# Gated values split in fp16 by channel scales and turned by DMAs instead of TensorE, with the forward transform in fp16 and the filling in another order

## What is computed

```python
# x: (8, 512, 512); in_proj_w: (1536, 512); wq_gate, wq_up: (1408, 512) int32; wq_down: (512, 1408) int32
u = transpose(x @ in_proj_w.T + in_proj_b, (0, 2, 1))
uc = depthwise_conv(u, short_w, taps=3, causal)[..., :512] + short_b
x0, x1, v = split(uc, 3, axis=1)
k = filter_k(...)                  # small sine network over positions, (512 channels, 512)
v = v * x1                         # "the gated values"
y = irfft(rfft(v, 1024) * rfft(k, 1024)) + v * filter_bias
y = transpose(y * x0, (0, 2, 1))
x = layernorm(x + y @ out_proj_w.T + out_proj_b)
gate, up = silu(qlinear(x, wq_gate)), qlinear(x, wq_up)
return layernorm(x + qlinear(gate * up, wq_down))
```

## Time and profile before

| | before |
|---|---|
| median of 3 runs (lowest to highest) | 991.51 us (990.58 to 991.9) |
| the profiled execution, own time | 990.85 us |
| its span | 989.0 us |
| busy: TensorE, VectorE, ScalarE, GpSimd | 96%, 77%, 44%, 56% of the span |
| granted TensorE clock, mean | 0.995 |
| first matmul of the first `gu` | 126.5 us |
| DMA, mean over the span | 48 GB/s |

### The profile page before, as it was taken

One profiled execution on the slowest core, in us unless ns is written; L12 is line 12 of the kernel. 1 busy time (PEld: TensorE's weight loads), 2 busy tenths in 40 slices (PEclk: granted clock), 3 DMA queues, 4 the chain that ended last, 5 costly groups with the idle time before them and its releaser, 6 DMA issues.

```text
span 989.0 us, 17316 instructions
## 1 busy us (share of the span) xinstructions
PE 951.5 (96%) x6121; PEld 666.5 (67%) x6210; DVE 763.5 (77%) x1441; ACT 436.7 (44%) x940; POOL 555.5 (56%) x628
## 2 busy tenths in 40 slices
PE   6798999999999999999999999999999999999996
PEld 3345667767676776767676676767767676787774
DVE  6698897787878788787887778787887878686454
ACT  4577543434344344534444343443445344334342
POOL 0269885474747656474765647475564747575210
PEclk9999999999999999999999999999999999999998
DMA  9444400221101211221012211012111110101100
GB/s 289 144 128 131 105 1 1 44 64 22 44 12 32 65 23 43 43 59 24 6 44 43 64 23 44 11 33 65 22 44 23 43 22 6 39 1 44 44 21 22
DMA packets 98953, 47.97 MB, mean 48 GB/s; under 512 B 80048, under 2 KB 84784, under 8 KB 98868
## 3 DMA queue, kind: packets, MB, share of 16 engines
q1 hardware_dynamic: 98370, 46.79, 18.2%
q10 hardware_dynamic: 498, 0.08, 0.0%
HBM read 32.17 MB, written 8.39 MB: 41 GB/s over the span
## 4 chain that ended last, share of the span: by engine, by line
PE 74%; DVE 9%; issue 6%; POOL 4%; ACT 3%; POOLq 0%; DVEq 0%; ACTq 0%
PE gate_up L1315 12%; PE gate_up L1316 12%; PE bank L1158 9%; PE bank L1160 9%; PE bank L1159 9%; PE down L1328 7%; PE down L1327 5%; PE bank L1275 4%; DVE tmp L1067 2%; PE spectrum L1158 1%; PE spectrum L1159 1%; PE spectrum L1160 1%; POOL acc L878 1%; DVE hid_lo L1146 1%; ACT cx L779 1%
## 5 line engine op out<-in xcount | busy, mean ns | idle before, releaser
L884 POOL TENSOR_TENSOR acc<-acc,tmp 128x256 f32<-128x256 f32 x160 | 122.5, 766 | 137.2 <-DVE tmp L1067 125.1
L1067 DVE TENSOR_TENSOR tmp<-spectrum,filt 128x512 f32<-128x512 f32 x256 | 172.7, 680 | 0.0
L830 ACT ACTIVATE hid<-gate_up,gate_scale 128x256 f32<-128x256 f32 x176 | 82.9, 471 | 195.6 <-PE gate_up L1316 195.5
L1315 PE MATMUL gate_up<-x2T_hi,wg_sb 128*128 128x256 f16 x704 | 163.3, 273 | 0.0
L1316 PE MATMUL gate_up<-x2T_lo,wg_sb 128*128 128x256 f16 x704 | 163.3, 273 | 0.0
L1316 PE MATMUL gate_up<-x2T_lo,wu_sb 128*128 128x256 f16 x704 | 163.3, 273 | 0.0
L1315 PE MATMUL gate_up<-x2T_hi,wu_sb 128*128 128x256 f16 x704 | 163.2, 272 | 0.0
L878 POOL TENSOR_TENSOR acc<-acc,tmp 128x512 f32<-128x512 f32 x96 | 125.2, 1304 | 56.1 <-DVE tmp L1067 55.9
L1158 PE MATMUL bank<-xT_hi,win_hi 128*128 128x512 f16 x360 | 137.6, 382 | 4.9 <-POOL win_lo L854 1.7
L1328 PE MATMUL down<-wd_sb,hid_lo 128*128 128x512 bf16 x352 | 133.4, 379 | 5.3
L837 ACT ACTIVATE hid_hi<-hid 128x256 f16<-128x256 f32 x176 | 73.4, 417 | 145.9 <-DVE hid L1140 145.9
(11 more groups left out here) (204 smaller groups left out, 1775.7 us busy)
## 6 DMA issues: line engine op xcount, KB each, us to landing
x<-in_x SPq DMA_DIRECT2D x28, 256.0 KB, 2.9
out<-x SPq DMA_DIRECT2D x28, 256.0 KB, 2.1
xstage<-in_x SPq DMA_DIRECT2D x96, 64.0 KB, 2.4
xstage<-in_x SPq DMA_DIRECT2D x12, 256.0 KB, 3.7
more_stages<-in_win SPq DMA_DIRECT2D x7, 256.0 KB, 5.1
x<-in_win SPq DMA_DIRECT2D x5, 256.0 KB, 5.0
acc<-in_decay SPq DMA_DIRECT2D x4, 256.0 KB
x2T_hi<-in_wu SPq DMA_DIRECT2D x4, 256.0 KB, 3.0
```

The costliest lines, as they stand in the source:

```text
L884: G.tensor_tensor(acc[:, i, 0, :], acc[:, i, 0, :], t[:, 1, :], ALU.subtract)
L1067: TT(dst, spectrum[j % 2][:, :, :], k_part, ALU.mult).then_inc(made_done, 1)
L1315: mm(dst, w[:, kb, rows(q)], x2T_hi[:, kb, ts], start=kb == 0, stop=False)
```

## The change

- The gated values get a scale per channel: `vmax` (VectorE: the greatest absolute value of each of the 256 channels, one instruction of 128x512 per channel group) and `vscale` (VectorE: four tiny instructions on 128x2, which make a power of two `v_scale` and its inverse over 2^10, `v_out`).
- `vsplit` now comes ahead of the turn: ScalarE writes `v_parts` hi as fp16 from `cv` times the scale, VectorE writes the low part (cv times the scale, less the high part), both from SBUF. SP then issues four DMA transposes per half into `vT_hi` and `vT_lo`, now fp16.
- `tv` is gone from TensorE and from the banks. `fw` waits for the transposes (`vt_in`).
- The forward matrix is held in fp16, hi and lo, scaled by 2^10 (ScalarE once, in the filling); `fw` multiplies fp16 by fp16.
- `y` undoes both scales: two instructions of 128x128 with the scalar `v_out` in the place of one of 128x256.
- `vmax` stands on beats 4 and 6 of a round, `vscale` on 6, `vsplit` on 7 and 8 (where the second group comes a beat later than the first).
- In the filling the steps `stage`, `net`, `turns`, `scales`, `spec` and the splits of the first halves stand in another order.

The diff, cut:

```diff
+FWD_FLOAT = 6
+FWD_SCALE = 2.0 ** 10
...
-    if beat in (7, 8) and ips and n not in (1, 2):
-        steps += [("tv", n, beat - 7)]
-    if beat == 6 and n in (1, 2):
-        steps += [("tv", n, 0), ("tv", n, 1)]
...
+    if beat in (7, 8) and n < HALVES:
+        steps += [("vsplit", n, beat - 7)]
...
+    if beat == 4 and n < HALVES:
+        steps += [("vmax", n, 0)]
+    elif beat == 6 and n < HALVES:
+        steps += [("vmax", n, 1), ("vscale", n)]
...
-STAGE_OF_BEAT = {2: (4, 5, 6), 7: (7, 8, 9, 10), 8: (11, 12, 13, 14), 9: (15, 16)}
+STAGE_OF_BEAT = {8: (7, 8, 9, 10, 11, 12), 9: (13, 14, 15, 16)}
...
-        steps += {2: [("net", 2), ("turns", 2), ("arg", 2)], 3: [("sin", 2)],
+        steps += {2: [("stage", 4), ("stage", 5), ("net", 2), ("turns", 2), ("arg", 2), ("stage", 6), ("sin", 2)],
                   4: [("kmm", d) for d in range(TB)]}.get(beat, [])
...
+    ("spec", 1, 0): [("ws", 2)],
+    ("spec", 1, 1): [("stage", k) for k in range(7, 11)],
+    ("v1", 0, 1): [("wmax", 7), ("wmax", 8), ("vmax", 0, 1), ("vscale", 0)],
+    ("spec", 0, 1): [("vsplit", 0, 0), ("vsplit", 0, 1)],
+    ("stage", 12): [("xmax", 1, tb) for tb in range(TB)],
+    ("acc", 1, 2, 2, 1): [("vmax", 2, 1), ("vscale", 2), ("vsplit", 2, 0), ("vsplit", 2, 1)],
...
-        fwd_hi, fwd_lo = (sb(f"fwd_{n}", [P, 2 * P], F32R) for n in ("hi", "lo"))
+        fwd_hi, fwd_lo = (sb(f"fwd_{n}", [P, 2 * P], F16) for n in ("hi", "lo"))
...
-        vT_hi, vT_lo = (sb(f"vT_{n}", [P, TB, W], F32R) for n in ("hi", "lo"))
+        v_parts = sb("v_parts", [P, 2, 2, L], F16)
+        v_inv, v_scale, v_out = (sb(f"v_{n}", [P, 2, 2], F32) for n in ("inv", "scale", "out"))
+        vT_hi, vT_lo = (sb(f"vT_{n}", [P, TB, W], F16) for n in ("hi", "lo"))
...
+                elif kind == "vsplit":
+                    n, c = at
+                    if n:
+                        sp.wait_ge(spectrum_ready, TB * n)
+                    for part, dst, done in ((0, vT_hi, v_hi_done), (1, vT_lo, v_lo_done)):
+                        sp.wait_ge(done, 2 * n + c + 1)
+                        sp.dma_start_transpose(dst[:, :, rows(c)], v_parts[:, c, part, :]).then_inc(vt_in, 16)
...
+                    elif k == FWD_FLOAT:
+                        A(floats[k][1], float_slot(k), ACT.Copy, scale=FWD_SCALE).then_inc(stage_hi, 1)
+                        act.wait_ge(stage_hi, k + 1)
+                        A(float_slot(k), float_slot(k), ACT.Copy, scale=FWD_SCALE).then_inc(fwd_scaled, 1)
...
-                        act.wait_ge(bank_ready, use["tv", n - 1, 1] + 1)
+                        act.wait_ge(v_lo_done, 2 * n)
...
                 elif kind == "vsplit":
-                    n, jp = at
-                    k = use["tv", n, jp]
-                    act.wait_ge(bank_ready, k + 1)
-                    if n > 0:
-                        act.wait_ge(spectrum_ready, TB * (n - 1) + 2 * jp + 2)
-                    A(flat(vT_hi[:, 2 * jp:2 * jp + 2, :]), bank_of(k), ACT.Copy).then_inc(v_hi_done, 1)
+                    n, c = at
+                    act.wait_ge(v_scaled, n + 1)
+                    if n:
+                        act.wait_ge(vt_in, 64 * n)
+                    A(v_parts[:, c, 0, :], cv[:, c, :], ACT.Copy, scale=v_scale[:, n % 2, c:c + 1]).then_inc(v_hi_done, 1)
...
+                elif kind == "vmax":
+                    n, c = at
+                    dve.wait_ge(v1_done, 2 * n + c + 1)
+                    greatest(v_inv[:, n % 2, c:c + 1], cv[:, c, :]).then_inc(v_max, 1)
+                elif kind == "vscale":
+                    n, = at
+                    least = v_inv[:, n % 2, :]
+                    dve.wait_ge(v_max, 2 * n + 2)
+                    TS(least.bitcast(I32), least.bitcast(I32), EXPONENT, None, ALU.bitwise_and).then_inc(v_step, 1)
+                    dve.wait_ge(v_step, 3 * n + 1)
+                    TS(least, least, LEAST_SUM, INTO_RANGE, ALU.max, ALU.mult).then_inc(v_step, 1)
+                    dve.wait_ge(v_step, 3 * n + 2)
+                    Vv.reciprocal(v_scale[:, n % 2, :], least).then_inc(v_scaled, 1)
+                    TS(v_out[:, n % 2, :], least, 1.0 / FWD_SCALE, None, ALU.mult).then_inc(v_step, 1)
                 elif kind == "vsplit":
-                    n, jp = at
-                    k = use["tv", n, jp]
-                    dve.wait_ge(v_hi_done, 2 * n + jp + 1)
-                    TT(flat(vT_lo[:, 2 * jp:2 * jp + 2, :]), bank_of(k), f32(flat(vT_hi[:, 2 * jp:2 * jp + 2, :])),
-                       ALU.subtract).then_inc(bank_read[bank_index[k]], 1)
+                    n, c = at
+                    dve.wait_ge(v_hi_done, 2 * n + c + 1)
+                    STT(out=v_parts[:, c, 1, :], in0=cv[:, c, :], scalar=v_scale[:, n % 2, c:c + 1], in1=v_parts[:, c, 0, :],
+                        op0=ALU.mult, op1=ALU.subtract).then_inc(v_lo_done, 1)
...
-                    TT(y, sums, y, ALU.mult).then_inc(bank_read[bank_index[k]], 1)
+                    dve.wait_ge(v_step, 3 * n + 3)
+                    for c in range(2):
+                        last = STT(out=y[:, c, :], in0=sums[:, c, :], scalar=v_out[:, n % 2, c:c + 1], in1=y[:, c, :],
+                                   op0=ALU.mult, op1=ALU.mult)
+                    last.then_inc(bank_read[bank_index[k]], 1)
...
-                elif kind == "tv":
-                    n, jp = at
-                    k = use["tv", n, jp]
-                    dst = free_bank(k)
-                    pe.wait_ge(v1_done, 2 * n + 2)
-                    for j in range(2):
-                        for c in range(2):
-                            last = nc.tensor.transpose(dst[:, (2 * j + c) * P:(2 * j + c + 1) * P], cv[:, c, rows(2 * jp + j)],
-                                                       ident[:, :])
-                    last.then_inc(bank_ready, 1)
                 elif kind == "fw":
                     n, j = at
                     k = TB * n + j
-                    pe.wait_ge(*read_of(use["tv", n, j // 2]))
+                    pe.wait_ge(vt_in, 64 * (n + 1))
```

More of the change, by code:

```diff
@@ L212, in setup_steps @@
             steps += [("wmax", k) for k in range(7, 13)]
-        elif beat == 6:
-            steps += [("wscale", 2), ("wtaps", 2)]
+        elif beat == 7:
+            steps += [("wscale", 2), ("wtaps", 2), ("scales", )]
         steps += [("stage", k) for k in STAGE_OF_BEAT.get(beat, ())]
-        if beat == 6:
-            steps += [("scales", )]
     if (n, beat) in SPEC_OF_BEAT:
@@ L229 @@
     ("wscale", 1): [("ip", 0, 1, 0)],
-    ("spec", 1, 1): [("ws", 2)],
-    ("vsplit", 0, 0): [("xmax", 1, tb) for tb in range(TB)],
+    ("spec", 1, 0): [("ws", 2)],
[4 more added lines that the diff above has]
+    ("acc", 1, 2, 2, 1): [("vmax", 2, 1), ("vscale", 2), ("vsplit", 2, 0), ("vsplit", 2, 1)],
     ("ip", 0, 1, 1): [("ip", 0, 0, 2)],
@@ L269 @@
     ("acc", 2, 3, 3, 1): [("op", 1, 1), ("ln1", 1, 1)],
-    ("silu", 0, 9): [("tv", 3, 1), ("dn", 0, 8)],
-    ("acc", 3, 0, 0, 0): [("vsplit", 3, 1)],
+    ("silu", 0, 9): [("dn", 0, 8)],
     ("acc", 3, 0, 0, 1): [("gu", 0, 10)],
@@ L312, in program @@
     steps += [("xsplit", 0, 2), ("xsplit", 0, 3), ("stage", 0), ("stage", 1), ("turns", 0), ("arg", 0), ("sin", 0), ("bias", )]
-    steps += [("wmax", k) for k in range(2, 6)] + [("net", 1), ("ws", 1), ("turns", 1), ("wtaps", 0), ("wscale", 1)]
-    steps += [("arg", 1), ("stage", 2), ("stage", 3), ("sin", 1), ("wtaps", 1), ("ws", 2)]
+    steps += [("wmax", k) for k in range(2, 6)] + [("ws", 1), ("net", 1), ("wtaps", 0), ("wscale", 1)]
+    steps += [("stage", 2), ("stage", 3), ("turns", 1), ("arg", 1), ("sin", 1), ("wtaps", 1), ("ws", 2)]
     steps += [("xmax", 1, tb) for tb in range(TB)]
@@ L340, in build @@
         steps = program()
-        use = count(steps, "xt", "ip", "tv", "iv", "op", "x2t")
+        use = count(steps, "xt", "ip", "iv", "op", "x2t")
         convs = count(steps, "conv")
@@ L424, in build @@
         v_hi_done, z_hi_done, z_lo_done = sem("v_hi_done"), sem("z_hi_done"), sem("z_lo_done")
+        v_max, v_step, v_scaled, v_lo_done, vt_in = (sem(n) for n in ("v_max", "v_step", "v_scaled", "v_lo_done", "vt_in"))
+        fwd_scaled = sem("fwd_scaled")
         res_biased, x2_hi_done, x2_lo_done = sem("res_biased"), sem("x2_hi_done"), sem("x2_lo_done")
@@ L854, in _ @@
                         G.tensor_tensor(floats[k][2], float_slot(k), floats[k][1], ALU.subtract).then_inc(x0_lo_done, 1)
+                    elif k == FWD_FLOAT:
+                        pool.wait_ge(fwd_scaled, 1)
+                        G.tensor_tensor(floats[k][2], float_slot(k), floats[k][1], ALU.subtract).then_inc(stage_used, 1)
                     elif k not in GROUP_OF_FLOAT:
```

5 lines of the change are left out of this document (2 added, 3 removed).

## The result

| | before | after |
|---|---|---|
| median (lowest to highest) | 991.44 us (990.58 to 991.9) | 1015.17 us (1013.82 to 1019.71) |
| ratio, 95% interval | | 1.0249 [1.0234, 1.0264] |
| profiled execution, own time; span | 990.85; 989.0 us | 1015.69; 1013.9 us |
| first gate/up matmul | 126.50 us | 139.02 us |
| from there to the start of the last unit | 848.60 us | 860.94 us |

The change costs 24 us where 2.7 us of gain were forecast. The two last lines, read from TensorE's timeline, say where: half in the filling, half in the middle.

A forecast was written before the change was run, and what follows sets the result against it. TensorE was taken to bound the long middle, with VectorE late in odd rounds and three engines near their end in the filling. 990.85 + 1.1 - 2.5 - 2.3 + 1.7 = 988.85, predicted as 988.8 us, range 980 to 996.

The forecast's parts named there:

- TensorE's relief: Turns gone and fp16 transform matmuls 0.11 us apart: 1.14 us per half, 14.8 over halves 3 to 15, as a ceiling.
- The place where VectorE holds TensorE: Middle rounds: down waits for VectorE's hid_lo, about 1.5 us in odd rounds, some 0.6 in even ones.
- The odd stretch: Odd rounds, VectorE nearly without pause from last projection's cx to eighth unit: two v_lo and one y add 0.35 us.
- the 2.0 us that the new order of the filling saves: Filling: filt is copied before the win_hi, so TensorE's 3.5 us wait shrinks and work starts 2.0 us earlier.
- Four tiny ones for the scale, 0.153 each as for x_inv: VectorE, each half: the scale's four small instructions, with waits between them, cost 0.75 us.
- the maxima and scales fall ahead of it, into VectorE's wait of 2.60 us: Odd rounds: maxima and scales fit VectorE's pause before x, so the busy stretch behind keeps its place.
- The rival of the port: Two SBUF inputs hold VectorE's low parts beside GpSimd: 996.5 us, decisive from a mean v_lo of 0.95; chance 0.20.
- +1.7, with bounds of -4 and +8: Filling, net: 7.0 us added on VectorE, less 3.3 covered by idle time, less 2.0 for an earlier start.
- Of these 7.0 us half of VectorE's 6.6 idle ones may cover 3.3: Filling: VectorE's added 7.0 us (5.6 of operations, 1.4 of slower v_lo) is partly hidden in its idle time.
- DMA ... I take nothing: Four transposes per half on SP's queue, 2.5 us from issue to landing, land before they are read: no cost.
- the rule of the Trainium skill that was weighed and put aside: 390 ns per 128x128 turn on TensorE, 1309 by DMA; advises TensorE where PSUM will do, so the change would lose.
- 1.1 - 2.5 - 2.3: Middle: five odd rounds +1.1 us, five even rounds -2.5, halves 14 and 15 -2.3; half 3 put at 0.

The follow-up runs named there:

- e3: The kernel before with only the new order of stage, net, turns, scales and weight maxima in the filling; 989.49 us, ratio 0.9984.
- e1: The kernel after with three of the scale's four small instructions split into one-column pieces, the reciprocal as it was; 1003.81 us, ratio to before 1.0129.
- e7: e1 with the first low part (vsplit) ahead of x's first ln1 in rounds 4 to 15; 1000.54 us.
- e8: e7 with constant scale 1 in halves 0 to 2, without maxima and scale there, and their y one instruction; 994.16 us.
- e9: e8 with the values of halves 1 and 2 turned by TensorE straight from cv, as in the kernel before; 986.99 us, ratio 0.9954.
- e10: e9 with the four xsplit steps of the next sequence a beat later in odd rounds from the fifth on; 984.57 us, ratio 0.9937.

## Why the prediction was wrong

**Right.** TensorE's relief. The transform's twelve matmuls start every 0.11 us in fp16, as taken from the gate/up (the first and the last of them, another between):

```profile
424.39 0.27 PE L1196 MATMUL spectrum<-vT_hi,fwd_hi 128*128 128x256 f16 x1
424.50 0.27 PE L1197 MATMUL spectrum<-vT_lo,fwd_hi 128*128 128x256 f16 x1
...
425.59 0.27 PE L1198 MATMUL spectrum<-vT_hi,fwd_lo 128*128 128x256 f16 x1
```

The place where VectorE holds TensorE, and the size: "the wait of a down for hid_lo in odd rounds grows from 0.3 to about 1.5 us, and one of some 0.6 appears in even ones" came as 1.39 and 0.77. An odd round in the kernel after (instruction, wait <- releaser):

```profile
421.05 0.66 DVE L1184 TENSOR_TENSOR hid_lo<-hid,hid_hi 128x256 f16<-128x256 f32 x1 [0.48 <-ACT hid_hi L855]
421.77 0.39 PE L1355 MATMUL down<-wd_sb,hid_hi 128*128 128x512 bf16 x1 [1.22 <-DVE hid_lo L1184]
```

The odd stretch of the earlier trace rows became 0.27 us longer (12.90 to 13.17, forecast 0.35), the even one 0.12 shorter (12.57 to 12.45, forecast some 0.2). Also right: the prices of the maxima, the low parts and y; the 2.0 us that the new order of the filling saves (e3: 1.8 in the total); that the rival by which the two SBUF inputs hold the low parts decides only from 0.95 us on (in the kernel after they took 0.745).

**The first step that failed** is "Four tiny ones for the scale, 0.153 each as for x_inv". The row was for 128x1; the new ones have 128x2, and three of them wait for GpSimd. With it fell "the maxima and scales fall ahead of it, into VectorE's wait of 2.60 us": that wait is for a GpSimd addition, beside which the scale takes 3.2 us. Price, by e1: 11.4 us, 11.0 of it in the middle. The trace of before had a nearer row, not read: the tensor_scalar on 128x2 that comes 32 times, whose least, median and greatest duration are

```profile
L1113 DVE TENSOR_SCALAR var_eps<-moments x32: 169/222/1078, 117.5 to 983.8; 128x2 f32<-128x2 f32 x32
```

The rival of the port was thus the right mechanism, but I gave it to the wide low parts and priced it by them, and the small instructions paid. The low parts are not free of it. Where they stand in the kernel after, they took 0.90 us at most; ahead of x in e7 0.96, and in e8 up to 1.78:

```profile
L1093 DVE SCALAR_TENSOR_TENSOR v_parts<-cv,v_scale,v_parts 128x512 f16<-128x512 f32 x32 | 28.0, 882 | 6.4 <-ACT v_parts L810 6.4
```

**The second** is the filling, "+1.7, with bounds of -4 and +8" (by its own terms -3.5 and +7.0). The loss is 12.5 us at the first gate/up, and 14.5 against the order alone, and two of the signs that were named for being wrong came: a transform that waits for a DMA, and a first gate/up after 132. Two terms were mis-sized. "Of these 7.0 us half of VectorE's 6.6 idle ones may cover 3.3": VectorE got 9.4 us more (busy until the first gate/up, by windows from 0: 100.8 us before, 110.2 after), for half 0's maxima and scale had been left out; and of what e8 takes away nothing was covered, for 5.2 us less work bring 5.5 us. And "DMA ... I take nothing", which was argued for the middle, was carried into the filling without a row: the transform there waited 7.0 us for two turns, the first behind four turns on SP, issued in 1.2 us each with a load of weights between them. By e8 and e9 the whole way by DMA is 9.6 us. TensorE's clock is part of these prices: granted at 0.50 from 88 to 98 us, the lower of its levels. It had fallen before the first of the two waits, when TensorE had stood still for 2.47 us behind a convolution of VectorE.

TensorE ahead of that wait, SP's issues in the kernel after from the first low part of half 1 on, and the transform:

```profile
88.19 1.12 PE L1266 MATMUL bank<-ident,xstage 128*128 128x128 f32 x4 [2.47 <-DVE cx L1064]
91.22 1.11 PE L1266 MATMUL gate_up<-ident,xstage 128*128 128x128 f32 x4 [1.92 <-DVE cx L1112]
...
89.11 1.24 SPq L676 DMA_TRANSPOSE vT_lo<-v_parts  x1
90.40 0.56 SPq L620 DMA_DIRECT2D x2T_lo<-in_wd  x1
91.08 1.20 SPq L676 DMA_TRANSPOSE vT_hi<-v_parts  x1
92.32 1.27 SPq L676 DMA_TRANSPOSE vT_lo<-v_parts  x1
...
94.89 0.39 PE L1196 MATMUL spectrum<-vT_hi,fwd_hi 128*128 128x256 f16 x1 [2.55 <-DMA vT_lo<-v_parts]
```

Here the rule of the Trainium skill that was weighed and put aside (VectorE: DVE Perf Modes, Rules for kernel authors: turn on TensorE where PSUM will do) holds, though for another reason than its figures: not the work of the DMA but its way was the cost, and only where nothing lay over it. In the middle no wait of the transform for a DMA is listed.

**The rest of the middle.** With the scale mended (e1) the middle is 849.95 against 848.60, so +1.35 where -3.7 was forecast (1.1 - 2.5 - 2.3). By the length of a round, e1 against before, the five even rounds make -0.21 us each in the mean and the five odd ones +0.59, where -0.50 and +0.21 were forecast. Of that 0.12 and 0.36 stand at the last unit, where gate/up waits for the turned x2T:

```profile
PE gate_up L1347 <- DMA x2T_lo<-parts: 2.9, 4, 1.0
```

In the last three even rounds, where that wait does not fall, the round makes -0.45; the odd ones make +0.23 without it. So VectorE's part was right to 0.1 us a round in the mean, and the DMA's "nothing" was wrong once more. For the odd rounds the mean is good to some 0.2 only, an estimate: singly they lie between -0.4 and +0.7. The remaining 1.8 us lie in the first and the last units: rounds 14 and 15 make -1.04 and -1.05, near their -1.14, but round 3 makes +0.90 and rounds 16 and 17 +0.65 together, where nothing was counted; why, no run shows. Why x2T lands later is open: all the turns go over one queue, and single issues of x2T_lo took up to 2.4 us in the kernel after where the longest before was 1.4, but no run separated the queue from VectorE's lateness.

**The version that beats both** is e10 at 984.57, with one thing less: in halves 0 to 2 it has no scale of its own. With every part of the computation in place the fastest is e3, at 989.49.

## What to carry to other kernels

Price a new small instruction by a row of the same operation, the same number of columns and the same neighbour on GpSimd, and look at least, median and greatest duration before the mean; two columns where there was one made 0.15 us into 1.2 beside a GpSimd at work. A step that moves from the bounding engine to a queue is free only where something lies over its latency: price it apart for the filling, by the issues and the landing in a row. When taking away one of two causes in a row shows nothing, take both away before dropping either.

## What the hardware showed that was not expected

- A tensor_scalar on 128x2 in SBUF that meets a GpSimd instruction ends with it (0.40 to 1.19 us, 41 of 48; the rest took 0.15 to 0.17). One on 128x1 never waits (0.133 to 0.155), nor does a reciprocal on 128x2 (0.165 to 0.167).
- The low part, 128x512 with two SBUF inputs, takes 0.74 us in the quiet start and up to 1.78 beside GpSimd's additions (e8). GpSimd pays too: its addition of 128x512 that met one ahead of x in e7 took 1.73 us, the one before it 1.26.
- In the kernel after TensorE's matmuls of 128x256 started every 0.21 us (95.08, 95.29, 95.50) behind its waits in the filling, instead of every 0.11: the granted clock was 0.50 from 88 to 98 us, the lower of TensorE's two levels, 1.2 instead of 2.4 GHz. TensorE had stood still from 85.7 to 88.2. Waits can thus cost more than their own length.
